# New orders for the calls of five engines in the scan part of a Mamba-2 and mixture-of-experts kernel

## The chip, the core and the metric

One core of a Trainium2 chip runs the whole program. The metric is the device time of one execution in microseconds (us). The engines are PE (TensorE, matrix products and transposes), DVE (VectorE), ACT (ScalarE), POOL (GpSimd) and SP (SyncE, which here issues most DMAs). Each engine works through its own instructions strictly in the order in which they are written; semaphores make one engine wait for another. A call that waits therefore also holds back everything written behind it on its engine.

## What is computed

Two Mamba-2 layers over 8 sequences of 512 tokens of width 256, with a residual around them and a layer norm behind, then a top-2 mixture of 8 experts. Cut to what matters here:

```python
for i in range(2):                                    # two layers
    res = h
    h = layernorm(h) * ln_w[i] + ln_b[i]
    z, xBC, dt = split(h @ in_w[i].T)
    dt = softplus(dt + dt_bias[i])
    xh, B, C = split(silu(causal_conv4(xBC) + conv_b[i]))
    # per head: state = exp(dt*A) * state + dt * x (outer) B ;  y = state . C
    y = scan(exp(dt * -exp(A_log[i])), dt, xh, B, C) + D[i] * xh
    y = y * silu(z)
    h = res + (y * rsqrt(mean(y*y) + eps) * rms_w[i]) @ out_w[i].T
x = layernorm(x + h)
x = layernorm(x + top2_experts(x))                    # 8 experts, gated by a softmax
```

## The kernel before

The scan part works in 16 **units**, one for each sequence and layer (units 0 to 7 are layer 0, 8 to 15 layer 1). A unit cuts its 512 tokens into four **chunks** `c[0]` to `c[3]` of 128 tokens; `c[4]` is chunk 0 of the next unit. While a unit's chunks are scanned, the same unit also does the input projection, convolution and layer norm of the next one (the "fills" `dt`, `c4`, `c0` to `c3`, `z0` to `z3`, `ln0`, `ln1`). Unit 0 runs the function `first`, units 1 to 8 run `plain`, units 9 to 14 run `routed`, which also routes the finished sequence to the experts (fills `t0`, `t1`, `lg`, `rk`), unit 15 runs `final`. Units 1 to 6 and 10 to 13 are loops in the program; 7, 8, 9 and 14 are written out. On every engine `plain` and `routed` are lists of calls, written by hand, and this list alone sets the order. The expert part follows from about 780 us on and isn't touched.

The calls on which the prediction rests, with the engine and the lines of the profile:

- PE `chunk_a` (L780) transposes a chunk's x into the PSUM bank `pt`; ACT `chunk_a` (L1252) copies it out to `xs`. PE `chunk_c` (L853) transposes the gated result `g` into the same bank `pt`; ACT `chunk_c` (L1257) copies the high half out, DVE `g_low` (L1678) makes the low half and frees the bank. There is one `pt`: its uses go strictly in the order a(1), c(0), a(2), c(1), a(3), c(2), a(4), c(3), each behind the one before.
- PE `chunk_cb` (L792), DVE `scan` (L1744, two instructions) and `chunk_mix` (L1752), PE `chunk_y` (L833) make the part of y from inside the chunk; PE `chunk_s` (L843) and `chunk_z` (L820), ACT `first_state` (L1315), DVE `next_state` (L1778) and `chunk_b1` (L1758) the part that comes through the state, all in the one bank `pz`. PE `chunk_d` (L871) is the output projection, ACT `chunk_d` (L1270) takes it out.
- POOL `x_dt` (L2621), `x_w` (L2629) and `x_d` (L2635) scale `xs` and so wait for ACT's copy; `old_state` (L2641); `add_xd` (L2647) adds `xd` to `y1` behind DVE `chunk_b1`. DVE `chunk_b2` (L1771) waits for `add_xd` and adds the part in PSUM. POOL `gated` (L2657) multiplies by silu(z) behind `chunk_b2`, and PE `chunk_c` waits for it.
- POOL `end` (L2584, L2585), ACT `end_scale` (L1278) and DVE `end_add` or, in plain units, `end_b` (L1719) finish the sequence of the unit before. POOL `scatter_before` (L2607) issues eight indirect DMAs in a routed unit. DVE `weigh` (L1735) and `taps` (L1705) prepare the next unit. POOL `add_x` (L2591), `rsqrt_ln` (L2578) and `u_low` (L2572) belong to the norms.
- SP loads the rows of `step_b` for each chunk (`spread_steps`, L525), which DVE `scan` waits for, and stores and loads the sequences (L550, L553, L559, L485).
- ACT functions come in table sets. `natural_log_exp_and_others` serves the softplus (L1231) and the exponentials of `steps` (L1241, L1242); the silu calls need another, and each change of set is an `ACT_TABLE_LOAD`.

## Time and profile before

| what | us |
|---|---|
| median of 3 runs (lowest, highest) | 1392.45 (1391.49, 1394.0) |
| the profiled execution | 1394.54 |
| its span, first to last instruction | 1392.5 |
| mean granted TensorE clock over the span | 0.966 |
| DVE busy, PE busy in the span | 1142.9, 1247.2 |
| a plain unit, mean of seven | 40.66 |
| a routed unit, mean of five | 46.20 |

The two unit lengths are distances between the starts of the call `weigh`, which runs once in each unit. PEclk or "clock" is the share of the full TensorE clock that was granted: 1.00 is 2.4 GHz, 0.50 is 1.2 GHz.

### The profile page before, as it was taken

The numbers are of one execution on the slowest core, as the hardware profiler recorded it, in microseconds if no ns is written. First come the engines' busy times: TensorE is split into PE (matmuls) and PEld (weight loads), VectorE is DVE, ScalarE is ACT, GpSimd is POOL, SyncE is SP. The second block draws the span as 40 slices with busy tenths as digits, with TensorE's granted clock in tenths as the row PEclk, the third lists the DMA queues.
The fourth block names the chain that finished last, engine by engine and source line by source line (L and its number), as shares of the span: only waits on it lengthen the run. The fifth ranks groups of instructions, "written<-read, shape, count | busy, mean of one in ns | idle before, by whom it ended". The sixth has DMA issues, their size and how long they took to land. (4 is left out here: it accounts for less than half of the span.)

```text
span 1392.5 us, 40595 instructions
## 1 busy us (share of the span) xinstructions
PE 1247.2 (90%) x13192; PEld 1024.2 (74%) x13193; DVE 1142.9 (82%) x2632; ACT 796.4 (57%) x1863; POOL 786.2 (56%) x743
## 2 busy tenths in 40 slices
PE   4889999999999999899977899999999999999980
PEld 2456666666666676676666789999999999999980
DVE  4889999999999999899986797869677967696656
ACT  5666666667666767576745434544545454445446
POOL 3467676677767787678776170707052707070771
PEclk9899999999999999899986999999999999999995
DMA  6213332334442323232224624232415241412554
GB/s 217 78 35 122 129 98 84 115 120 136 137 133 88 112 62 127 84 103 68 96 103 121 172 68 118 79 114 68 117 45 143 59 123 45 143 42 59 149 145 155
DMA packets 120721, 146.63 MB, mean 105 GB/s; under 512 B 47745, under 2 KB 103553, under 8 KB 120513
## 3 DMA queue, kind: packets, MB, share of 16 engines
q1 hardware_dynamic: 109504, 102.15, 24.5%
q0 software_dynamic: 10848, 42.32, 9.9%
q10 hardware_dynamic: 288, 1.19, 0.2%
q8 instruction: 39, 0.64, 0.2%
q14 instruction: 42, 0.34, 0.1%
HBM read 98.83 MB, written 37.47 MB: 98 GB/s over the span
## 5 line engine op out<-in xcount | busy, mean ns | idle before, releaser
L1111 PE MATMUL pe<-arena 128*128 128x128 f16 x3408 | 216.8, 221 | 25.7 <-issue 15.1
L1111 PEld LDWEIGHTS pe<-arena 128*128 128x128 f16 x3408 | 200.2, 99 | 33.0 <-issue 29.9
L1111 PE MATMUL pa<-arena 128*128 128x128 f16 x3408 | 215.3, 220 | 2.1 <-issue 1.1
L1111 PEld LDWEIGHTS pa<-arena 128*128 128x128 f16 x3408 | 197.9, 98 | 2.6 <-issue 1.3
L1136 PE MATMUL py<-arena 128*128 (+1 forms) x1704 | 197.6, 273 | 2.1 <-DVE arena L2363 2.1
L1572 ACT ACTIVATE arena<-pe,arena 128x128 f32<-128x128 f32 x568 | 161.2, 370 | 57.3 <-PE pe L1111 57.0
L1705 DVE SCALAR_TENSOR_TENSOR arena<-pa,arena 128x511 f32<-128x511 f32 (+2 forms) x240 | 178.7, 745 | 11.3 <-ACT arena L1209 5.2
L1136 PEld LDWEIGHTS py<-arena 128*128 128x128 f16 x1704 | 163.5, 98 | 20.3 <-issue 2.6
L1744 DVE TENSOR_TENSOR_SCAN arena<-arena,pe 128x512 f32<-128x512 f32 x128 | 148.7, 1203 | 3.2 <-issue 1.8
L2557 POOL TENSOR_SCALAR arena<-arena 128x1536 f16<-128x1536 f32 (+2 forms) x35 | 45.1, 1288 | 167.6 <-DVE arena L2363 152.5
L833 PEld LDWEIGHTS py<-arena 128*128 128x128 f32 x1024 | 124.2, 197 | 17.9 <-issue 9.1
L833 PE MATMUL py<-arena 128*128 128x64 f32 x1024 | 129.5, 281 | 1.5 <-DVE arena L1752 1.0
L686 PE MATMUL pa<-arena 128*128 128x512 f16 x480 | 120.9, 393 | 9.6 <-DVE arena L1705 9.5
L2657 POOL TENSOR_TENSOR arena<-arena 128x512 f32<-128x512 f32 x64 | 88.5, 1383 | 66.5 <-DVE arena L1771 66.4
L2315 DVE SCALAR_TENSOR_TENSOR pm<-pa,arena 128x128 f32<-128x128 f32 x284 | 80.3, 350 | 52.5 <-ACT arena L1572 48.7
L1578 ACT ACTIVATE arena<-pm 128x512 f16<-128x512 f32 x71 | 42.4, 597 | 131.0 <-DVE pm L2315 131.0
L2315 DVE SCALAR_TENSOR_TENSOR pz<-pa,arena 128x128 f32<-128x128 f32 x284 | 80.3, 351 | 32.9 <-ACT arena L1572 32.0
L871 PE MATMUL pm<-arena 128*128 128x256 f16 x768 | 100.2, 283 | 7.8 <-DVE arena L1678 7.1
L1578 ACT ACTIVATE arena<-pz 128x512 f16<-128x512 f32 x71 | 42.4, 597 | 111.6 <-DVE pz L2315 111.6
L694 PE MATMUL pa<-arena 128*128 128x512 f16 x384 | 95.0, 390 | 3.4 <-ACT arena L1198 2.0
L871 PEld LDWEIGHTS pm<-arena 128*128 128x128 f16 x768 | 76.6, 102 | 25.6 <-DVE arena L1678 10.2
L2847 POOL DMA_INDIRECT arena<-answer,arena x64 | 61.2, 956 | 54.6 <-issue 54.6
(306 smaller groups left out, 2535.8 us busy)
## 6 DMA issues: line engine op xcount, KB each, us to landing
arena<-step_rows SPq DMA_DIRECT2D x64, 512.0 KB, 6.0
arena<-in_w_exp POOLq DMA_DIRECT2D x32, 768.0 KB, 4.9
arena<-queue SPq DMA_DIRECT2D x74, 129.5 KB
answer<-arena SPq DMA_DIRECT2D x71, 128.0 KB, 1.7
arena<-in_x SPq DMA_DIRECT2D x16, 512.0 KB, 6.5
answer<-zeros SPq DMA_DIRECT2D x10, 512.0 KB, 4.8
arena<-h SPq DMA_DIRECT2D x9, 512.0 KB, 6.1
h<-arena SPq DMA_DIRECT2D x8, 512.0 KB, 3.0
```

What stands on the lines that cost most here:

```text
L686: ins = pe.matmul(bank[:, :], win[:, l, b, d, OX + c * P:OX + (c + 1) * P], uT[:, vq, a, d, :], start=(n == 0), stop=(n == len(passes) - 1))
L694: ins = pe.matmul(bank[:, :], uT[:, vq, a, d, k * P:(k + 1) * P], win[:, l, b, d, 0:DI], start=(n == 0), stop=(n == len(passes) - 1))
L833: ins = pe.matmul(py[:, h * HD:(h + 1) * HD], mix[:, kq, h, :], dtx[:, kq, h, :], start=True, stop=True)
L871: ins = pe.matmul(OUT, gT[:, c.kq, a, t, :], wout[:, c.layer, b, t, :], start=(n == 0), stop=(n == len(passes) - 1))
L1111: ins = pe.matmul(bank[:, f * P:(f + 1) * P], w_split[:, p, hl, d * 2 * FF + col:d * 2 * FF + col + P], x_hl[:, r, x, d * P:(d + 1) * P], ...
L1136: ins = pe.matmul(py[:, 0:D], a[:, b, f, :], part(p, hl, W1N + f * D, D), start=(half == 0 and n == 0), stop=(half == 1 and n == len(passe ...
L1572: ins = e.activation(sg[:, half, f, :], GATE[half][:, f * P:(f + 1) * P], ACT.Silu, bias=b1a[:, bass.ds(ex_, 1), ff], scale=1.0 / S1)
L1578: e.activation(acth[:, r, 4 * half:4 * half + 4].rearrange("p f t -> p (f t)"), GLU[half][:, :], ACT.Copy).then_inc(hi_done[half], 1)
L1705: ins = dve.scalar_tensor_tensor(acc[:, mq, s:T], pa[bank][:, 0:T - s], cw[:, l, ct, TAPS - 1 - s:TAPS - s], acc[:, mq, s:T], ALU.mult, AL ...
L1744: dve.tensor_tensor_scan(flat[:, h * T:(h + 1) * T], step_b[:, c.k, h * T:(h + 1) * T], IDENT4[:, :], 0.0, ALU.mult, ALU.add).then_inc(sca ...
L2315: ins = dve.scalar_tensor_tensor(GLU[half][:, f * P:(f + 1) * P], VALUE[half][:, f * P:(f + 1) * P], b1v[:, bass.ds(ex_, 1), ff], sg[:, ha ...
L2657: pool.tensor_tensor(g[:, kq], y2[:, kq], zs[:, c.q, k].rearrange("p (h d) -> p h d", h=NH), ALU.mult).then_inc(g_ready, 1)
```

## The change

The lists `plain` and `routed` get new orders on all five engines. SP's loop over the units is taken apart into `first_unit`, `plain_unit` and `routed_unit` for this. No call does other work; three waits are added where the new orders need them (ACT `chunk_a` also waits for `dtx_ready` and `xw_ready`, POOL `x_d` waits for ACT's copy itself), and the loading of the logarithm table becomes a call of its own, `log_table`. The core of the diff, with both lists of POOL whole:

```diff
@@ SP, plain_unit @@
+                store_steps(u + 1)
+                load_hres(u)
+                if u + 3 <= MAMBA_UNITS:
+                    load_hln(u + 3)
+                clear(u)
+                spread_steps(u + 1, 0)
+                store_h(u)
+                spread_steps(u + 1, 1)
+                spread_steps(u + 1, 2)
+                store_hx(u)
+                spread_steps(u + 1, 3)
@@ PE, plain @@
+                chunk_cb(c[2])
+                chunk_c(c[0])
                 do_fills(st, ["c1"])
-                chunk_c(c[0])
-                chunk_s(c[1])
                 chunk_y(c[1])
                 do_fills(st, ["c2"])
+                chunk_d(c[0])
+                chunk_cb(c[3])
                 chunk_a(c[2])
-                chunk_z(c[2])
-                chunk_d(c[0])
-                chunk_cb(c[2])
-                do_fills(st, ["c3"])
-                chunk_s(c[2])
+                chunk_s(c[1])
                 turn_b(st.u + 1, 1 - st.q, c[0].n + 1)
                 chunk_c(c[1])
...
@@ PE, routed @@
+                chunk_y(c[0])
+                chunk_cb(c[2])
+                chunk_a(c[1])
+                do_fills(st, ["c0"])
+                chunk_c(c[0])
+                do_fills(st, ["c1"])
+                steps(st.u + 1, 1 - st.q)
+                chunk_z(c[1])
...
@@ ACT, routed @@
+                first_state(c[0])
+                log_table()
+                conv_first(st, "c4")
+                chunk_a(c[1])
+                softplus(st)
+                conv_first(st, "c0")
+                end_scale(st)
+                chunk_c(c[0])
+                conv_silu(st, "c4")
+                conv_silu(st, "c0")
+                steps(st)
+                conv_first(st, "c1")
+                chunk_a(c[2])
+                conv_first(st, "c2")
+                conv_silu(st, "c1")
...
@@ DVE, plain @@
+                ln_stats(st.u + 2, st.h + 1, st.q)
                 scan(c[1])
                 dt_first(st)
                 chunk_mix(c[1])
+                chunk_b2(c[0])
...
+                scan(c[2])
+                g_low(c[0])
+                chunk_mix(c[2])
+                chunk_b2(c[1])
+                taps(st, "c1", ch1)
+                next_state(c[1])
+                taps(st, "c2", ch1)
+                chunk_b1(c[2])
+                taps(st, "c3", ch1)
+                ch1.close()
                 weigh(st)
+                g_low(c[1])
+                next_state(c[2])
+                chunk_b2(c[2])
...
@@ DVE, routed @@
+                taps(st, "c0", ch1)
+                end_add(st)
+                chunk_b1(c[1])
...
+                chunk_mix(c[4])
                 g_low(c[3])
-                chunk_mix(c[4])
+                weigh(st)
@@ POOL, x_d @@
                 n, kq = c.n, c.kq
+                pool.wait_ge(pt_free, c.use("a") + 1)
                 at_least(pool, y_free, n - 1)
@@ POOL, plain @@
-                x_d(c[1])
-                add_xd(c[1])
-                old_state(c[2])
-                gated(c[1])
-                x_w(c[2])
-                x_dt(c[2])
-                add_x(st)
-                x_d(c[2])
...
+                old_state(c[1])
+                end(st)
                 gated(c[0])
                 x_dt(c[1])
+                x_w(c[1])
+                rsqrt_ln(st.u + 2)
                 x_d(c[1])
+                x_d(c[2])
                 add_xd(c[1])
+                gated(c[1])
+                x_dt(c[2])
+                x_w(c[2])
                 old_state(c[2])
+                x_d(c[3])
                 add_xd(c[2])
                 gated(c[2])
                 x_dt(c[3])
                 add_xd(c[3])
                 gated(c[3])
                 x_w(c[4])
                 x_dt(c[4])
                 u_low(st.u + 2, st.q, st, "ln0")
                 u_low(st.u + 2, st.q, st, "ln1")
+                add_x(st)
+                x_d(c[4])
@@ POOL, routed @@
+                x_d(c[1])
+                scatter_before(st, 0, 1)
+                end(st)
+                old_state(c[1])
+                gated(c[0])
+                add_xd(c[1])
+                x_dt(c[1])
+                x_w(c[1])
+                scatter_before(st, 1, 2)
+                x_d(c[2])
+                rsqrt_x1(st)
+                x_dt(c[2])
+                gated(c[1])
...
+                add_xd(c[3])
+                x_d(c[4])
+                scatter_before(st, 6, 7)
+                scatter_before(st, 7, 8)
+                gated(c[3])
+                u_low(st.u + 2, st.q, st, "ln0")
+                u_low(st.u + 2, st.q, st, "ln1")
+                x_w(c[4])
+                x_dt(c[4])
```

How the instructions stand before and after, at three places. The lines of the kernel after are shifted by 45 to 54.

**POOL in unit 8, the last plain one, before.** From `gated` of chunk 0 on:

```order
L2657 TENSOR_TENSOR arena<-arena 128x512 [waits pt_free,ss_ready,y_free]
L2621 TENSOR_TENSOR arena<-arena 128x512 [waits y_full,pt_free]
L2635 TENSOR_TENSOR arena<-arena 128x512 [waits y_free]
L2647 TENSOR_TENSOR arena<-arena 128x512 [waits xd_ready,z_free]
L2641 TENSOR_TENSOR arena<-arena 128x256 [waits z_free]
L2657 TENSOR_TENSOR arena<-arena 128x512 [waits pt_free,ss_ready,y_free]
L2629 TENSOR_TENSOR arena<-arena 128x512 [waits z_full,wdt_ready,pt_free]
L2621 TENSOR_TENSOR arena<-arena 128x512 [waits y_full,pt_free]
L2591 TENSOR_TENSOR arena<-arena 128x1024 [waits h_ready]
L2635 TENSOR_TENSOR arena<-arena 128x512 [waits y_free]
```

The same stretch of POOL after the change (`gated` is L2712 now, `x_dt` L2675, `x_w` L2683, `rsqrt_ln` L2632, `x_d` L2690, `add_xd` L2702, `old_state` L2696):

```order
L2712 TENSOR_TENSOR arena<-arena 128x512 [waits pt_free,ss_ready,y_free]
L2675 TENSOR_TENSOR arena<-arena 128x512 [waits y_full,pt_free]
L2683 TENSOR_TENSOR arena<-arena 128x512 [waits z_full,wdt_ready,pt_free]
L2632 TENSOR_TENSOR arena<-arena,half_neg 128x4 [waits ln_done,ln_var]
L2633 TENSOR_TENSOR arena<-arena 128x4 [waits ln_pow]
L2690 TENSOR_TENSOR arena<-arena 128x512 [waits y_free,pt_free] x2
L2702 TENSOR_TENSOR arena<-arena 128x512 [waits xd_ready,z_free]
L2712 TENSOR_TENSOR arena<-arena 128x512 [waits pt_free,ss_ready,y_free]
L2675 TENSOR_TENSOR arena<-arena 128x512 [waits y_full,pt_free]
L2683 TENSOR_TENSOR arena<-arena 128x512 [waits z_full,wdt_ready,pt_free]
L2696 TENSOR_TENSOR arena<-arena 128x256 [waits z_free]
```

`x_d` of chunks 1 and 2 now stand together ahead of `add_xd` of chunk 1; before, `x_d` of chunk 2 stood six calls behind it.

**PE in unit 8, before** (`chunk_c` of chunk 0, `chunk_s`, `chunk_y`, the fill `c2`, `chunk_a` of chunk 2):

```order
L853 MATMUL pt<-ident,arena 128x128 [waits pt_free,g_ready]
L853 MATMUL pt<-ident,arena 128x128 x3
L843 MATMUL pz<-arena 64x256 [waits bs_ready,z_free,xw_ready]
L843 MATMUL pz<-arena 64x256
L833 MATMUL py<-arena 128x64 [waits y_free,dtx_ready,m_done]
L833 MATMUL py<-arena 128x64 x7
L686 MATMUL pa0<-arena 128x512 [waits a_free0]
L686 MATMUL pa0<-arena 128x512 x5
L780 MATMUL pt<-ident,arena 128x128 [waits pt_free]
```

and after (`chunk_y`, the fill, `chunk_d` of chunk 0, `chunk_cb` of chunk 3, `chunk_a` of chunk 2, `chunk_s`):

```order
L878 MATMUL py<-arena 128x64 [waits y_free,dtx_ready,m_done]
L878 MATMUL py<-arena 128x64 x7
L731 MATMUL pa0<-arena 128x512 [waits a_free0]
L731 MATMUL pa0<-arena 128x512 x5
L916 MATMUL pm<-arena 128x256 [waits ex_ready,out_free,pt_free]
L916 MATMUL pm<-arena 128x256 x11
L837 MATMUL pe0<-arena 128x128 [waits m_done]
L825 MATMUL pt<-ident,arena 128x128 [waits pt_free]
L825 MATMUL pt<-ident,arena 128x128 x3
L888 MATMUL pz<-arena 64x256 [waits bs_ready,z_free,xw_ready]
```

`chunk_d` of chunk 0 and a `chunk_cb` now stand ahead of `chunk_a` of chunk 2.

**POOL at the start of unit 14, the last routed one, before** (`end`, three scatters, `x_w`, `x_dt`, `gated` of chunk 0):

```order
L2584 TENSOR_SCALAR arena<-arena 128x4 [waits ss_ready]
L2585 TENSOR_TENSOR arena<-arena,half_neg 128x4 [waits sve_ready]
L2607 DMA queue<-arena 34304x259 [waits slot_ready,x1_ready]
L2607 DMA queue<-arena 34304x259 x2
L2629 TENSOR_TENSOR arena<-arena 128x512 [waits z_full,wdt_ready,pt_free]
L2621 TENSOR_TENSOR arena<-arena 128x512 [waits y_full,pt_free]
L2657 TENSOR_TENSOR arena<-arena 128x512 [waits pt_free,ss_ready,y_free]
```

and after:

```order
L2690 TENSOR_TENSOR arena<-arena 128x512 [waits y_free,pt_free]
L2661 DMA queue<-arena 34304x259 [waits slot_ready,x1_ready]
L2638 TENSOR_SCALAR arena<-arena 128x4 [waits ss_ready]
L2639 TENSOR_TENSOR arena<-arena,half_neg 128x4 [waits sve_ready]
L2696 TENSOR_TENSOR arena<-arena 128x256 [waits z_free]
L2712 TENSOR_TENSOR arena<-arena 128x512 [waits pt_free,ss_ready,y_free]
L2702 TENSOR_TENSOR arena<-arena 128x512 [waits xd_ready,z_free]
L2675 TENSOR_TENSOR arena<-arena 128x512 [waits y_full,pt_free]
L2683 TENSOR_TENSOR arena<-arena 128x512 [waits z_full,wdt_ready,pt_free]
```

`x_d` of chunk 1 (it waits for ACT's copy of that chunk) now stands ahead of `end`, and `add_xd` of chunk 1 ahead of `x_dt`.

## Rows read from the trace of the kernel before

**Rows 1.** Busy time by unit: length; PE, PEld, DVE, ACT, POOL; clock, DMA, GB/s.

```profile
271.95:313.02 41.07, 38.53 (x277) 26.80 (x277) 38.21 (x61) 26.46 (x53) 28.32 (x28) 1.00 0.37 115
...
483.97:528.86 44.89, 41.61 (x306) 30.25 (x306) 42.63 (x111) 31.31 (x63) 36.06 (x36) 1.00 0.31 105
528.86:579.39 50.53, 45.16 (x302) 32.48 (x301) 43.51 (x110) 30.69 (x62) 35.98 (x36) 0.90 0.35 112
```

**Rows 2.** DVE `weigh` in time order: start, us, instruction; first and last of each stretch.

```profile
108.93 0.33 DVE L1735 TENSOR_TENSOR arena<-arena 128x32 f32<-128x32 f32 x1 [0.40 <-ACT arena L1242]
...
393.52 0.40 DVE L1735 TENSOR_TENSOR arena<-arena 128x32 f32<-128x32 f32 x1 [0.17 <-ACT arena L1242]
439.14 0.18 DVE L1735 TENSOR_TENSOR arena<-arena 128x32 f32<-128x32 f32 x1
...
670.12 0.18 DVE L1735 TENSOR_TENSOR arena<-arena 128x32 f32<-128x32 f32 x1
```

**Rows 3.** A plain unit in time order, single calls of DVE, PE, ACT, POOL.

```profile
274.55 0.68 DVE L1678 SCALAR_TENSOR_TENSOR arena<-pt,arena 128x512 f16<-128x512 f32 x1
281.12 1.21 DVE L1752 TENSOR_TENSOR arena<-arena,pe 128x1024 f32<-128x1024 f32 x1
...
275.29 0.65 PE L780 MATMUL pt<-ident,arena 128*128 128x128 f32 x4 [0.72 <-DVE arena L1678]
...
277.18 1.47 PE L871 MATMUL pm<-arena 128*128 128x256 f16 x12
278.59 0.48 PE L792 MATMUL pe<-arena 64*128 64x128 f32 x2
...
276.11 0.59 ACT L1252 ACTIVATE arena<-pt 128x512 f32<-128x512 f32 x1
...
270.93 1.04 POOL L2635 TENSOR_TENSOR arena<-arena 128x512 f32<-128x512 f32 x1
285.87 1.28 POOL L2647 TENSOR_TENSOR arena<-arena 128x512 f32<-128x512 f32 x1
```

**Rows 4.** DVE `taps` and `scan`, 100 to 500 us: busy us, mean ns | idle.

```profile
L1705 DVE SCALAR_TENSOR_TENSOR arena<-pa,arena 128x511 f32<-128x511 f32 x150 | 111.6, 744 | 3.7
L1744 DVE TENSOR_TENSOR_SCAN arena<-arena,pe 128x512 f32<-128x512 f32 x76 | 88.3, 1202 | 0.7
```

**Rows 5.** Routed units in time order: POOL scatter and `end`, PE, ACT `end_scale`.

```profile
475.81 1.01 POOL L2607 DMA_INDIRECT queue<-arena  x1 [0.16 <-issue]
...
510.17 1.49 PE L871 MATMUL pm<-arena 128*128 128x256 f16 x12 [0.99 <-DVE arena L1678]
...
516.86 1.46 PE L686 MATMUL pa<-arena 128*128 128x512 f16 x6
...
511.49 1.04 POOL L2585 TENSOR_TENSOR arena<-arena,half_neg 128x4 f32<-128x4 f32 x1
...
515.85 1.71 ACT L1278 ACTIVATE arena<-arena 128x256 f32<-128x256 f32 x4
```

**Rows 6.** ACT, a change of table set in a plain unit, and what follows.

```profile
271.68 1.28 ACT L1220 ACT_TABLE_LOAD   x1
272.97 0.63 ACT L1220 ACTIVATE arena<-arena 64x512 f32<-64x512 f32 x1
```

**Rows 7.** PE's idle stretches in time order, with their length in brackets.

```profile
91.48 0.66 PE L853 MATMUL pt<-ident,arena 128*128 128x128 f32 x4 [2.27 <-POOL arena L2657]
...
568.40 1.11 PE L853 MATMUL pt<-ident,arena 128*128 128x128 f32 x4 [2.61 <-POOL arena L2657]
...
706.25 1.09 PE L709 MATMUL pa<-ident,arena 128*128 128x128 f32 x8 [2.73 <-DVE arena L1728]
```

**Rows 8.** One-us stretches for PE: busy, granted clock, DMA, GB/s.

```profile
567.00:568.00 1.00, 0.00 (x0) 0.73 0.00 0
...
577.00:578.00 1.00, 1.00 (x8) 0.65 0.94 350
```

**Rows 9.** DMA issues by kind: KB each, median us to landing.

```profile
arena<-step_rows SPq DMA_DIRECT2D x64, 512.0 KB, 6.0
```

More of the change, by code:

```diff
@@ L1358, in first @@
                 chunk_a(c[1])
+                log_table()
                 softplus(st)
@@ new lines, in plain @@
+                taps(st, "c1", ch1)
[4 more added lines that the diff above has]
+                ch1.close()
+                weigh(st)
+                g_low(c[1])
+                next_state(c[2])
+                chunk_b2(c[2])
+                scan(c[3])
+                chunk_b1(c[3])
+                chunk_mix(c[3])
+                end_b(st)
+                chunk_b2(c[3])
+                g_low(c[2])
@@ new lines, in plain, with routed @@
+                scan(c[4])
+                chunk_mix(c[4])
+                g_low(c[3])
+            def routed(st):
+                c = [Chunk(st, k) for k in range(NK + 1)]
+                scan(c[1])
+                chunk_mix(c[1])
+                dt_first(st)
+                scan(c[2])
+                chunk_b2(c[0])
+                ch1 = Chain(dve, c_dve2, S1_LINKS, st.u + 1)
+                taps(st, "c4", ch1)
+                dt_last(st, ch1)
+                taps(st, "c0", ch1)
+                end_add(st)
+                chunk_b1(c[1])
+                ch3 = s3_stats(st)
@@ L2014, in plain @@
+                scan(c[3])
+                next_state(c[2])
                 chunk_b2(c[2])
-                next_state(c[2])
-                scan(c[3])
                 chunk_mix(c[3])
+                s3_top(st, ch3)
                 chunk_b1(c[3])
+                s3_place(st, ch3)
                 g_low(c[2])
@@ L2021, in plain @@
                 scan(c[4])
+                chunk_mix(c[4])
                 g_low(c[3])
[L2023 to L2062 removed]
+                weigh(st)
             def final(st):
@@ L2772, in routed @@
                 x_dt(c[4])
-                x_d(c[4])
                 u_low(st.u + 2, st.q, st, "ln0")
                 u_low(st.u + 2, st.q, st, "ln1")
+                add_x(st)
+                x_d(c[4])
+            def routed(st):
+                c = [Chunk(st, k) for k in range(NK + 1)]
+                x_d(c[1])
[11 more added lines that the diff above has]
+                gated(c[1])
+                scatter_before(st, 2, 3)
+                x_w(c[2])
+                rsqrt_ln(st.u + 2)
+                old_state(c[2])
+                scatter_before(st, 3, 4)
+                add_xd(c[2])
+                gated(c[2])
+                scatter_before(st, 4, 5)
+                x_dt(c[3])
+                x_d(c[3])
+                scatter_before(st, 5, 6)
+                add_xd(c[3])
[7 more added lines that the diff above has]
+                x_dt(c[4])
             def final(st):
```

350 lines of the change are left out of this document (138 added, 212 removed).

## The prediction, written before the result was known

> **What bounds the kernel now.** I read the busy times by unit first. A plain unit is 41.07 us long; DVE is busy for 38.21 of it and PE for 38.53, at clock 1.00 [rows 1]. A routed unit is 44.89 with DVE at 42.63 and PE at 41.61 [rows 1]. So two engines are nearly full, and together with the strict order on each engine that bounds the gain from above and leaves the loss open: DVE has 2.86 us of idle time in a plain unit and 2.26 in a routed one, and a new order can take away no more than that, but can add any wait. The starts of `weigh` give the lengths: 7 plain units in 393.52 - 108.93 = 284.59, 40.66 each, and 5 routed ones in 670.12 - 439.14 = 230.98, 46.20 each [rows 2]. One of the five is 50.53 with clock 0.90, where the others are near 45 [rows 1].
>
> I lay the new lists against each other, each call with its duration from a row, counting time from the first DVE call of a unit. What has to be looked for is a call that now stands behind another that waits for something later.
>
> **Plain units, first wait.** POOL's `add_xd` of chunk 1 now stands behind `x_d` of chunk 2, which needs ACT's copy of chunk 2. PE's `chunk_a` of chunk 2 waits for the bank `pt`, which DVE `g_low` of chunk 0 frees, and on PE `chunk_d` of chunk 0 (it waits for the same `g_low`) and a `chunk_cb` now stand ahead of it. From the start of `g_low`: 0.68, then PE 1.47 + 0.48 + 0.65, ACT's copy 0.59, `x_d` 1.04, `add_xd` 1.28 [rows 3], 6.2 in all, and with some 0.05 for each of five hand-overs (PE starts 0.06 after `g_low` ends, 274.55 + 0.68 against 275.29 [rows 3]) 6.4. DVE has only `g_low` and `chunk_mix`, 0.68 + 1.21 [rows 3], less a small overlap, to do before `chunk_b2` of chunk 1, which waits for `add_xd`: 1.8. **DVE waits 4.6.**
>
> **Second wait.** The same pattern for chunk 2: `add_xd` stands behind `x_d` of chunk 3, whose `chunk_a` waits for `g_low` of chunk 1, with nothing ahead of it this time: 0.68 + 0.65 + 0.59 + 1.04 + 1.28 = 4.2 [rows 3], 4.5 with hand-overs; DVE has `g_low` and `next_state`, 0.9. **3.6.** Elsewhere in the unit I find 0.4 (the first `taps` wait for `conv_first`, since PE has `chunk_s` and `chunk_y` ahead of the fill `c4`). DVE's calls keep their time, so the unit is 41.07 - 2.86 + 4.6 + 3.6 + 0.4 + 0.3 (its waits for its own results) = 47.1; the 0.8 that every second unit is shorter goes half into the waits, and I take 47.0 for all. Eight units: 8 x (47.0 - 40.66) = **+51**.
>
> **SP** now issues the step rows of chunks 1 and 2 behind the store of h, which waits for `end_b`. They land 6.0 later [rows 9]. From the end of `end_b` to the next `scan` of chunk 1 DVE has `chunk_b2`, two `g_low`, a scan pair, `chunk_mix` and `ln_stats`, 7.5 by my layout, and SP needs 0.8 to get to them. That hides them by 0.7; a landing 2 us late would cost 1.3 in each of eight units, +10, which I keep for the range. `weigh` and `add_x` move to late places, where nobody waits for them.
>
> **Routed units, first wait.** POOL now begins with `x_d` of chunk 1, so a scatter, `end`, `old_state` and `gated` of chunk 0 all stand behind ACT's copy of chunk 1. On PE the seven calls from `chunk_d` to `chunk_y` take 516.86 - 510.17 = 6.7 [rows 5]; `chunk_cb` and the transpose behind them and ACT's copy bring the copy to 8.0. Then `x_d` 1.0, a scatter 1.2, `end` 1.3 and ACT's `end_scale` 1.71 [rows 3, 5]: ready at 13.6. DVE has until `end_add` two scan pairs, one `chunk_mix`, two `taps` of three instructions (1.20 and 0.74 each [rows 4]) and small calls: 11.9. **DVE waits 1.8.**
>
> **Second.** `gated` of chunk 0 is done at 13.8 (`end` 11.9, `old_state` 0.6, 1.28 [rows 3]). PE has had nothing to do since the fill `c0` at 8.7, because `chunk_c` of chunk 0 is next: **5.2 us idle**. Behind it stand the fill `c1`, `steps` and `chunk_z`, some 3.7 more. `chunk_b1` of chunk 1 starts at 17.7 where DVE was ready at 14.8. **2.9.** `gated` of chunk 1 likewise sits behind `x_d` of chunk 2 and `x_dt`, which leaves PE idle for 2.9.
>
> **Third.** At the end `gated` of chunk 3 stands behind `x_d` of chunk 4 and two scatters. The copy of chunk 4, behind ACT's `ln_out`, is there at 49.7; + 1.0 + 2 x 1.2 + 1.3, + PE 0.65, + ACT 0.6 with hand-overs gives `g_low` of chunk 3 at 56.2, where DVE was done at 51.5. **4.7**, with PE idle for 4.6. Four small waits (`chunk_mix`, `g_low` and `chunk_b1` of chunk 1 and 2, `s3_place`) add 2.7. Sum 12.1, and 44.89 + 12.1 = 57.0; unit 9 has no scatters, 3.6 less. Six units: 5 x 57.0 + 53.4 - 6 x 46.20 = **+61**. If all of the idle 2.26 went, 14 less.
>
> **ACT's tables.** In `routed` the exponentials of `steps` now stand between silu calls: two more loads in each unit, 2 x 1.28 [rows 6]. `conv_first` of `c1` is ready at 21.4 by my layout and DVE comes to it at 22.3, so they are hidden, with 0.9 to spare; without that cover they are 2.6 x 6 = 15. The row after a load starts 0.01 behind its end [rows 6]. The Trainium skill (ScalarE: Activation LUTs, "What ACT_TABLE_LOAD costs") adds a drain of about 1.38 to each switch; by that rule the sum would be some 19 us more (an estimate from that page: 1.0 in each plain unit, 1.9 in each routed one). The row shows no drain, and I go by the row.
>
> **The clock.** This is the second large term. When PE had been idle for 2.61 and for 2.73, the clock fell to 0.50 [rows 7]; after the first it fell in 567 to 568 and came back in 577 to 578, with PE busy throughout from 568.4 [rows 7, 8]. After 2.27 it did not fall [rows 7]. The unit of the first fall took 50.53 against 44.89, 5.6 more [rows 1]. The new lists leave PE idle for 4.7 in each plain unit (from `turn_b` to `chunk_c` of chunk 1, through the first wait), and for 5.2, 2.9 and 4.6 in each routed one. Each fall makes PE's work of the next 7 to 9 us twice as long, and behind all of these gaps it is on the path to DVE's next call. I take 3.5 for a plain unit (PE's calls up to `chunk_a` of chunk 3, 7 us, at half speed for 7) and 2 x 3.7 for a routed one, leaving the gap of 2.9 out: 8 x 3.5 + 6 x 7.4 = **+72**.
>
> **Sum.** 51 + 61 + 72 = +184 on the profiled execution's 1394.54: 1578.5. The median of the runs is 2.1 below it, so **1576**.
>
> **The rivals.**
> *The clock holds.* The waits are as above, but no gap meets the clock's fall. For: a gap of 2.27 went by without one [rows 7]. Against: both gaps over 2.6 shown did not, and these are up to twice as long. It gives 1392 + 112 = 1504.
> *More falls.* The routed gap of 2.9 also counts (4.3 x 6 = 26) and PE's two gaps around `chunk_c` of chunk 2 in a plain unit, 1.6 and 1.8 with little between, bring a second fall there (4.4 x 8 = 35): 1602 to 1637.
> *Faster.* The point is POOL's `x_d` of chunk 2 in plain units. If the copy of chunk 2 is there when POOL comes to it, `add_xd` isn't late, DVE's idle 2.86 shrinks to its own 0.4 in each plain unit, and the routed units keep their length: 8 x -2.4 = -19, 1373. It decides where the wait at `chunk_b2` of chunk 1 is under 2.9; I get 4.6 from durations alone, with one `pt` bank, so this needs an error of mine in the order.
> *The waits overlap.* In a chain of five engines a wait may take the place of a later one; with half of the waits gone and no fall of the clock it is about 1450.
>
> **How the numbers follow.** 0.60 for the forecast, 0.17 for the clock that holds, 0.14 for more falls, 0.04 for faster or no change, 0.05 for overlapping waits. The forecast's own terms carry an error of 1.5 us in each unit, +-20. The range reaches from the second case less 14 to the lower half of the third: 1490 to 1630. 0.2% is 2.8 us, about what a measurement of this kernel can tell from no change. Faster 0.03, same 0.01, slower 0.96.
>
> **What would show it.** In the profile after: `weigh` 50 to 51 us apart in plain units and 64 in routed ones (47 and 57 with the clock at 1.00); DVE's largest wait is `chunk_b2` for `add_xd`, some 8 us in each plain unit; `g_low` for ACT and `chunk_b1` for PE in routed units; PE's idle time before `chunk_c` for `gated`, 4 to 5 us at a time; a clock clearly under 0.97 between 100 and 800 us; the expert part as long as before. Wrong would be: `add_xd` without a late `x_d` ahead of it, DVE still 90% busy in plain units, or a clock of 1.00 behind gaps of 4 us.

## The result, and the profile of the changed kernel

The changed kernel takes 1562.9 us (median of 4 runs, 1562.4 to 1565.3), the kernel before, on the same chip, 1393.2: a ratio of 1.122, 95% interval 1.120 to 1.124. The forecast was 1576 with a range of 1490 to 1630. The profiled execution took 1562.42 with a span of 1560.7. In the later comparisons the kernel before had 1393.3 to 1394.1.

The page of the changed kernel: busy time of each engine, and the granted clock in 40 slices of the span.

```profile
PE 1312.3 (84%) x13192; PEld 1070.8 (69%) x13193; DVE 1155.6 (74%) x2632; ACT 819.3 (52%) x1875; POOL 779.4 (50%) x743
...
PEclk9998898988898999887888869999999999999996
```

The kernel before has 1247.2 for PE, 1142.9 for DVE and 796.4 for ACT. PE's matmuls are longer at the lower clock; ACT has 12 more instructions, the table loads (15 us); DVE has the same 2632 instructions and is busy for 12.7 more, 9.1 of it in the two small instructions of `ln_stats` that the last section is about; the rest is a balance of other small ones. Of the first 24 digits 15 are under 9, where 4 were: the falls lie in the scan part; the expert part behind them is as it was, 638.3 from its first product to the end in both kernels. The 170 us came mostly as waits. The engines by stretch, a plain unit and three of the five routed ones (length; busy PE, and in the plain unit PEld, DVE, ACT, POOL too; clock, DMA share, GB/s), which answer to [rows 1]:

```profile
275.85:326.94 51.09, 43.24 (x278) 30.52 (x277) 37.18 (x61) 27.43 (x53) 28.10 (x27) 0.87 0.29 93
...
552.53:611.63 59.10, 45.01 (x306) 0.90 0.23 82
611.63:671.81 60.18, 47.14 (x309) 0.87 0.23 80
671.81:737.45 65.64, 51.09 (x309) 0.81 0.20 65
```

`weigh` starts seven periods from 125.12 to 480.04, 50.70 us each (before 40.66), and five from 552.53 to 863.51, 62.2 each (before 46.2 [rows 2]). The routed units come in two lengths, 59.1 to 60.3 three times and 65.6 and 65.8, and the longer ones have the lower clock (0.81 and 0.79).

DVE's waits in the plain unit from 275.85 to 326.94, summed by pair (total, times, longest); before, the largest wait of this kind was under 1 us:

```profile
DVE arena L1825 <- POOL arena L2702: 8.0, 2, 4.5
DVE arena L1732 <- ACT arena L1307: 2.0, 1, 2.0
DVE arena L1812 <- PE pz L865: 1.8, 1, 1.8
DVE arena L1825 <- PE py L878: 1.3, 1, 1.3
```

One unit from its chunk 1 to its chunk 3, across the late `weigh` at 275.85, first POOL, then DVE, then PE (start, length, instruction, idle time in front of it and its releaser). L2690 is `x_d` of chunk 2 and L1302 ACT's copy of that chunk, L2702 `add_xd`, L2712 `gated`; L1825 is `chunk_b2`, L1812 `chunk_b1`, L1806 `chunk_mix`, L1732 `g_low` and L1307 ACT's `chunk_c`; L898 is PE's `chunk_c`, L878 `chunk_y`, L865 `chunk_z`:

```profile
263.51 1.04 POOL L2690 TENSOR_TENSOR arena<-arena 128x512 f32<-128x512 f32 x1 [5.84 <-ACT arena L1302]
...
265.81 0.69 DVE L1825 TENSOR_TENSOR arena<-py,arena 128x512 f32<-128x512 f32 x1 [4.50 <-POOL arena L2702]
273.01 0.69 DVE L1812 TENSOR_TENSOR arena<-pz,arena 128x512 f32<-128x512 f32 x1 [1.74 <-PE pz L865]
280.44 0.69 DVE L1825 TENSOR_TENSOR arena<-py,arena 128x512 f32<-128x512 f32 x1 [3.48 <-POOL arena L2702]
288.15 0.69 DVE L1825 TENSOR_TENSOR arena<-py,arena 128x512 f32<-128x512 f32 x1 [1.30 <-PE py L878]
295.07 0.69 DVE L1732 SCALAR_TENSOR_TENSOR arena<-pt,arena 128x512 f16<-128x512 f32 x1 [1.96 <-ACT arena L1307]
...
268.06 1.11 PE L898 MATMUL pt<-ident,arena 128*128 128x128 f32 x4 [4.36 <-POOL arena L2712]
282.68 0.65 PE L898 MATMUL pt<-ident,arena 128*128 128x128 f32 x4 [1.45 <-POOL arena L2712]
285.13 2.89 PE L878 MATMUL py<-arena 128*128 128x64 f32 x16 [1.79 <-DVE arena L1806]
```

And PE's granted clock around them, in stretches of 3 us (length, PE busy, clock, DMA share, GB/s):

```profile
265.00:268.00 3.00, 0.00 (x0) 0.59 0.00 0
268.00:271.00 3.00, 2.94 (x9) 0.50 0.00 0
271.00:274.00 3.00, 3.00 (x12) 0.77 0.00 0
274.00:277.00 3.00, 3.00 (x25) 1.00 0.00 0
...
283.00:286.00 3.00, 1.21 (x12) 1.00 0.00 0
286.00:289.00 3.00, 3.00 (x17) 0.50 0.39 137
...
292.00:295.00 3.00, 3.00 (x24) 0.86 0.34 137
```

POOL's `x_d` of chunk 2 waits 5.84 for ACT's copy, `add_xd` of chunk 1 runs behind it (264.51 to 265.77), and `chunk_b2` starts at 265.81. PE stands still for 4.36 us and its clock falls from the 2.4 to the 1.2 GHz level; it stands still for 1.45 and 1.79 with one short call between, and the clock falls again. The waits for PE and ACT (1.74, 1.30, 1.96) stand behind the falls, each of those for POOL (4.50, 3.48) ahead of one.

A routed unit, in the same form; L1782 is `end_add`, L1328 ACT's `end_scale`, L837 `chunk_cb`:

```profile
615.71 1.22 DVE L1806 TENSOR_TENSOR arena<-arena,pe 128x1024 f32<-128x1024 f32 x1 [1.65 <-PE pe L837]
626.69 1.23 DVE L1782 TENSOR_TENSOR arena<-arena 128x1024 f32<-128x1024 f32 x1 [1.80 <-ACT arena L1328]
632.31 0.69 DVE L1812 TENSOR_TENSOR arena<-pz,arena 128x512 f32<-128x512 f32 x1 [4.40 <-PE pz L865]
671.20 0.69 DVE L1732 SCALAR_TENSOR_TENSOR arena<-pt,arena 128x512 f16<-128x512 f32 x1 [4.80 <-ACT arena L1307]
...
626.66 1.11 PE L898 MATMUL pt<-ident,arena 128*128 128x128 f32 x4 [4.97 <-POOL arena L2712]
635.53 1.97 PE L878 MATMUL py<-arena 128*128 128x64 f32 x16 [1.97 <-issue]
643.76 0.66 PE L898 MATMUL pt<-ident,arena 128*128 128x128 f32 x4 [1.54 <-POOL arena L2712]
669.42 1.11 PE L898 MATMUL pt<-ident,arena 128*128 128x128 f32 x4 [4.57 <-POOL arena L2712]
```

### The profile page after: what moved, and what is told of

Its sections match the earlier page's. It is cut to its first block and busy times, and to the rows that moved or that the text cites. A ratio compares the mean times of both kernels' runs of the same rounds, so it can differ in the third digit from the quotient of the medians.

```text
span 1560.7 us, 40707 instructions
## 1 busy us (share of the span) xinstructions
PE 1312.3 (84%) x13192; PEld 1070.8 (69%) x13193; DVE 1155.6 (74%) x2632; ACT 819.3 (52%) x1875; POOL 779.4 (50%) x743
## 5 line engine op out<-in xcount | busy, mean ns | idle before, releaser
L878 PE MATMUL py<-arena 128*128 128x64 f32 x1024 | 139.7, 295 | 25.8 <-DVE arena L1806 14.7
L878 PEld LDWEIGHTS py<-arena 128*128 128x128 f32 x1024 | 134.6, 210 | 37.2 <-issue 17.6
L2690 POOL TENSOR_TENSOR arena<-arena 128x512 f32<-128x512 f32 x64 | 66.6, 1041 | 184.4 <-ACT arena L1302 184.4
L898 PE MATMUL pt<-ident,arena 128*128 128x128 f32 x256 | 50.2, 329 | 119.3 <-POOL arena L2712 118.2
L731 PE MATMUL pa<-arena 128*128 128x512 f16 x480 | 138.4, 432 | 2.0 <-DVE arena L1759 2.0
L898 PEld LDWEIGHTS pt<-ident,arena 128*128 128x128 f32 x256 | 33.6, 165 | 132.8 <-issue 88.4
L916 PE MATMUL pm<-arena 128*128 128x256 f16 x768 | 119.1, 317 | 6.0 <-DVE arena L1732 5.7
L2369 DVE SCALAR_TENSOR_TENSOR pm<-pa,arena 128x128 f32<-128x128 f32 x284 | 80.2, 350 | 52.7 <-ACT arena L1626 49.2
L2712 POOL TENSOR_TENSOR arena<-arena 128x512 f32<-128x512 f32 x64 | 83.3, 1301 | 63.4 <-DVE arena L1825 63.1
L916 PEld LDWEIGHTS pm<-arena 128*128 128x128 f16 x768 | 87.8, 117 | 34.3 <-DVE arena L1732 12.1
L1825 DVE TENSOR_TENSOR arena<-py,arena 128x512 f32<-128x512 f32 x64 | 43.9, 686 | 81.6 <-POOL arena L2702 66.8
```

The lines of the kernel that those rows point to most:

```text
L731: ins = pe.matmul(bank[:, :], win[:, l, b, d, OX + c * P:OX + (c + 1) * P], uT[:, vq, a, d, :], start=(n == 0), stop=(n == len(passes) - 1))
L878: ins = pe.matmul(py[:, h * HD:(h + 1) * HD], mix[:, kq, h, :], dtx[:, kq, h, :], start=True, stop=True)
L898: ins = pe.transpose(pt[:, t * P:(t + 1) * P], gk[:, t * P:(t + 1) * P], ident[:, :])
L916: ins = pe.matmul(OUT, gT[:, c.kq, a, t, :], wout[:, c.layer, b, t, :], start=(n == 0), stop=(n == len(passes) - 1))
L2369: ins = dve.scalar_tensor_tensor(GLU[half][:, f * P:(f + 1) * P], VALUE[half][:, f * P:(f + 1) * P], b1v[:, bass.ds(ex_, 1), ff], sg[:, ha ...
L2690: pool.tensor_tensor(xd[:, kq], xs[:, kq], by_head(dsk[:, c.layer]), ALU.mult).then_inc(xd_ready, 1)
```

## The experiments

The theory is that of the prediction: a call of POOL that waits for a late copy of ACT now stands ahead of one that others need, PE idles behind it, its clock falls, and DVE waits again for the slower PE. What has to be told apart is which kind of unit pays, whether POOL's order alone does it, and how much is the clock's.

### One kind of unit alone

The first run has the old lists of all engines in routed units, the second has them in plain units; the other kind is new.

> The kernel after, with all five lists of the routed units in their old order; the plain units keep the new one. My theory (each kind of unit has waits and falls of the clock of its own, about 10.0 us in each of 8 plain units, 16 in each of 6 routed ones as the two traces put them, 50.7 against 40.7 and 62.2 against 46.2): plain units stay at 50 to 51, routed ones go back to 45 to 46, time 1393 + 80 = 1473 (1465 to 1482). Rival, that the kinds of unit feed each other's delays across their border (calls of chunk 4 are late, the clock stays low): the routed units stay above 50 and the time is above 1500.

> The kernel after, with all five lists of the plain units in their old order; the routed units keep the new one. My theory: plain units 40.7, routed ones 62, time 1393 + 6 x 16, less a little for unit 9, = 1483 (1472 to 1492), and what this and the kernel with plain units alone lose sums to the whole loss of 170 within 6. Rival, feeding across the border: the two losses sum to clearly less or more than 170.

Measured: 1471.0 (ratio 1.055, 1.053 to 1.057) and 1482.9 (1.065, 1.063 to 1.067). The two losses, 77.7 and 89.7, add up to 167.4, where both together lose 169.6. Within these intervals the two losses simply add: eight plain units lose 9.7 us each, six routed ones 15.0. (That an edit of one kind can still change single units of the other shows further down.)

### POOL's two calls in plain units, taken back and put in

In the first kernel only POOL's list of plain units is edited, all else is the changed kernel:

```
                 x_d(c[1])
-                x_d(c[2])
                 add_xd(c[1])
                 gated(c[1])
+                x_d(c[2])
...
-                x_d(c[3])
                 add_xd(c[2])
                 gated(c[2])
+                x_d(c[3])
```

> The kernel after with one change: in POOL's plain list x_d of chunk 2 and of chunk 3 stand behind add_xd and gated of the chunk before, not ahead of them; all other lists as they are. My theory (these two calls make DVE wait 4.0 twice, and the PE gap behind the first brings the fall of the clock): both waits of DVE for add_xd fall to under 1, the clock is 1.00 in plain units, a plain unit goes from 50.7 to 39.5 to 42.5, time 1563 - 8 x 9.5 = 1487 (1475 to 1505). Rival one, PE's order is the cause (chunk_d and chunk_cb ahead of chunk_a): the wait moves to another call (x_dt for chunk_y, gated for chunk_c) and the unit stays above 47, time above 1530. Rival two, the new DVE order with end_b late and ln_stats first: the unit stays near 50.

Measured: 1487.1 (1.068, 1.063 to 1.074), 76 below the changed kernel and the time of the run with only the routed units new. A plain unit of it (columns as above):

```profile
241.48:282.43 40.95, 38.39 (x277) 26.71 (x277) 39.75 (x61) 27.01 (x53) 28.03 (x27) 1.00 0.36 116
```

The clock is at 1.00 and DVE waits for POOL no more. The second kernel is the kernel before, with the one edit the other way round:

```
                 x_d(c[1])
+                x_d(c[2])
                 add_xd(c[1])
...
                 add_x(st)
-                x_d(c[2])
```

> The kernel before with one edit, on POOL in plain units: x_d of chunk 2 ahead of add_xd of chunk 1 (and the wait on pt_free in front of it, which x_dt had done for it). Theory (the order of POOL alone makes the first wait): add_xd(1) now queues behind a copy of xs that ACT makes only after PE's taps, so DVE's chunk_b2(1) waits 3.5 to 4.5 us where it waited none, PE gets a gap of 4 us or more ahead of chunk_c(1) and the granted clock falls behind it; plain units go from 40.7 to 43.7 to 47, the time to 1415 to 1443. Rival (the wait needs the new order of the other engines too, which reach chunk_a(2) later in the new plain unit): under 1 us per unit, at most 1400.

Measured: 1440.3 (1.033, 1.031 to 1.035), plain units 46.0 to 47.6. POOL, DVE and PE in it (L2636 is `x_d`, L2648 `add_xd`, L1771 `chunk_b2`, L820 `chunk_z`), and PE's clock:

```profile
300.97 1.04 POOL L2636 TENSOR_TENSOR arena<-arena 128x512 f32<-128x512 f32 x1 [4.80 <-ACT arena L1252]
301.97 1.26 POOL L2648 TENSOR_TENSOR arena<-arena 128x512 f32<-128x512 f32 x1
...
303.26 0.69 DVE L1771 TENSOR_TENSOR arena<-py,arena 128x512 f32<-128x512 f32 x1 [4.87 <-POOL arena L2648]
...
304.34 1.95 PE L820 MATMUL pz<-arena 128*128 128x256 f32 x4 [5.15 <-DVE arena L1778]
...
301.00:304.00 3.00, 0.00 (x0) 1.00 0.55 171
...
305.00:308.00 3.00, 3.00 (x14) 0.51 0.00 0
```

The whole chain stands here in five rows: `x_d` waits 4.80 for the copy, `add_xd` runs behind it, `chunk_b2` waits 4.87, PE 5.15, and then the clock falls. PE's gap is ahead of `chunk_z`, not of `chunk_c` as I had written. One call too early costs 6 us in each of eight units, in a kernel that is otherwise as it was. PE's new order, whose `chunk_d` and `chunk_cb` the forecast counts ahead of the copy, is not needed for it.

### The clock by itself

The changed kernel with matmuls whose results nobody reads, so that PE doesn't idle; no wait is taken away. In the first kernel 34 of them (128x256) stand behind `turn_b`, in the second also 10 ahead of `chunk_c(c[2])` and 14 ahead of `chunk_y(c[3])`.

```
                 turn_b(st.u + 1, 1 - st.q, c[0].n + 1)
+                filler(34)
                 chunk_c(c[1])
...
+                filler_c(c[2], 10)
                 chunk_c(c[2])
+                filler_y(c[3], 14)
                 chunk_y(c[3])
```

> The kernel after with 34 matrix products of 128x256 f16 (about 0.11 us each at the full clock, 3.7 in all) added on PE in each plain unit, behind turn_b and ahead of chunk_c of chunk 1, which is where PE is idle for 4.4; their results go to a part of a PSUM bank that nobody reads. They separate the wait from the clock. My theory: the clock stays at 1.00 in plain units where the gap of 4.4 alone made it fall, a plain unit goes from 50.7 to 47 to 48, time 1563 - 8 x 3.5 = 1535 (1525 to 1547). Rival, the clock costs nothing here since DVE waits for POOL anyway: 1563 within 5. If the falls come from the later gaps instead, the clock stays low and the time too: 1555 to 1570.

> The changed kernel with matmuls whose results nobody reads in plain units, in the three gaps of TensorE: 34 (128x256) behind turn_b, 10 ahead of chunk_c(2), 14 ahead of chunk_y(3). Nothing is taken from any wait. Theory: the two falls of the granted clock in a plain unit come of the gaps; with all three filled the clock stays at its upper level and the unit is 50.7 less 1.7 (the wait for chunk_z) and less 2.5 to 3.3 (the waits for chunk_y(3) and chunk_c(3)): 46 to 47, the time 1520 to 1535 (with the first gap alone filled it was 1550.6 at 47.9). Rival (the second pair of waits is the order's, not the clock's): it stays at 47.9 and 1550.

Measured: 1550.6 (1.110, 1.105 to 1.116) and 1562.5 (1.120, 1.118 to 1.122). Units of the first and of the second kernel, in the columns of [rows 1]; the last two lines are routed ones of the second:

```profile
223.04:270.93 47.89, 43.48 (x311) 31.10 (x311) 37.18 (x60) 27.25 (x53) 28.01 (x27) 0.96 0.32 99
...
272.76:320.81 48.05, 45.07 (x335) 32.26 (x335) 38.52 (x60) 27.12 (x53) 28.01 (x27) 1.00 0.31 99
...
610.55:675.76 65.21, 50.88 (x309) 36.49 (x307) 44.46 (x111) 34.43 (x65) 35.31 (x36) 0.81 0.21 74
675.76:736.40 60.64, 47.45 (x309) 33.48 (x307) 45.13 (x111) 34.50 (x65) 35.31 (x36) 0.87 0.21 70
```

The fillers did in most units to the clock what they should. With the first alone one fall is left in six of the seven units counted. With all three none is left in four of the seven, and the waits of 1.74, 1.30 and 1.96 are gone there but for 0.4; the other three still show one fall (clock 0.93 to 0.97), without an idle stretch of PE over 1 us ahead of it. In the unit shown two waits over half a microsecond are left at the clock of 1.00, 3.73 and 4.51, both for `add_xd`: these are the order's own.

But this unit takes 48.05 and the mean of the seven is 49.2 (48.0 to 51.0), where 46 to 47 was expected. The three waits had made 5.0; DVE is busy for 1.3 more than in the changed kernel's unit (the last section tells where), the waits for `add_xd` have grown by 0.3, and small gaps by 0.5. And the time is not lower, because the routed units, whose code is not touched, took 60.6 once and 64.3 to 65.5 four times, where the changed kernel has three near 60 and two near 66. So the rival's number came (1562.5, even above its 1550), but not by its reason.

The 1535 expected of the first kernel was too low because five of its units take 47.9, 2.8 less than the mean of 50.7 and not 3.5, and the other two 49.5 and 50.7.

### POOL's order in routed units

The start of the unit:

```
+                end(st)
+                old_state(c[1])
+                gated(c[0])
                 x_d(c[1])
                 scatter_before(st, 0, 1)
-                end(st)
-                old_state(c[1])
-                gated(c[0])
                 add_xd(c[1])
```

> The changed kernel with POOL's routed unit re-ordered at its start: end, old_state and gated(0) first, then x_d(1) and the scatter. Theory: end_add's wait (1.80 us) and the PE gap ahead of chunk_c(0) (4.97) go, with them the fall of the clock behind the gap and so most of DVE's wait for chunk_z at chunk_b1(1) (4.40): routed units 62.2 -> 56 to 58, the time 1526 to 1540. Rival (PE has other work to catch up, so chunk_z still is late, or the time comes back at the third wait): 1550 to 1563.

Measured: 1524.8 (1.093, 1.092 to 1.095), 38 lower. Routed units are 53.1 to 56.5 long instead of 62.2; the wait at `end_add` is gone, and that at `chunk_b1` of chunk 1 too, where it was 3.8 to 5.6. In the first of the five, DVE instead waits 1.51 for ACT's `conv_first` and 0.93 for `chunk_z` at `chunk_b1` of chunk 2. The end of the unit:

```
+                gated(c[3])
                 x_d(c[4])
                 scatter_before(st, 6, 7)
                 scatter_before(st, 7, 8)
-                gated(c[3])
```

> The changed kernel with gated(3) on POOL in routed units ahead of x_d(4) and the last two scatters. Theory: DVE's wait of 4.4 to 4.8 us at g_low(3) shrinks to under 1 us and PE's gap of 4.6 ahead of chunk_c(3) goes: 62.2 -> 57 to 58 per routed unit, the time 1532 to 1542. Rival (what is saved there is waited for at the start of the next unit, since x_d(4), its x_w and x_dt and the scatters come that much later): 1555 to 1563.

Measured: 1554.8 (1.113, 1.108 to 1.117), 8 lower where the full wait would be 29. The rival's range, 1555 to 1563, begins just above it. PE of this kernel at the head of one unit, and further on DVE (L2626 is POOL's `u_low`):

```profile
615.09 0.76 PE L723 MATMUL pa<-arena 128*128 128x8 f16 x24 [1.97 <-POOL arena L2626]
...
616.00:621.00 5.00, 5.00 (x17) 0.50 0.01 3
621.00:626.00 5.00, 5.00 (x21) 0.50 0.00 0
...
657.71 0.69 DVE L1812 TENSOR_TENSOR arena<-pz,arena 128x512 f32<-128x512 f32 x1 [3.64 <-PE pz L865]
```

The wait of 4.8 at `g_low` is gone, as meant. But `u_low` now is late for PE's fill `dt`, the clock falls there, and further on DVE waits 3.64 for `chunk_z` at `chunk_b1` of chunk 2, behind a fall that lasts 11 us in both units of this kernel that I read. In the changed kernel such a long one stands in the unit of 65.64 but not in that of 60.18. What was saved at the end of one unit is largely waited for in the next: units of 58.9, 64.9, 61.0, 61.8, 56.7.

All three edits of POOL together, the other engines' new lists kept:

> The changed kernel with all three repairs of POOL's order together: in plain units x_d(2) and x_d(3) behind add_xd and gated of the chunk before; in routed units end and gated(0) ahead of x_d(1), and gated(3) ahead of x_d(4). The other four engines keep the new order. Theory (nearly all of the loss is POOL's order and the falls of the clock behind its gaps): the two single repairs that worked add up, 1562.9 less 76 less 38 = 1449, and the third brings 8 (what it brought alone) to 29 (its full wait): 1420 to 1441. Rival (the second half of the routed unit is set by other things, as when the third repair stood alone): 1441 to 1455.

Measured: 1423.7 (1.020, 1.018 to 1.023). POOL's calls in four places, and the falls of the clock behind them, make 139 of the 170 us. Together the three bring more than each alone: 76 + 38 + 8 would be 1441, and 17 more came. Which pair of them does that was not tried. The rest, 30 us, is in the routed units (48.9 to 53.8, before 46.2), where DVE's waits for PE are 3.3 at most; what makes it was not tried.

### What the new plain units are worth without that fault

> The new plain units with POOL's x_d(2) and x_d(3) moved back, and the old routed units on all engines. By adding up the single runs: 1471 less 76 = 1395, the same as the kernel before (plain units 41.0 where the kernel before has 40.7).

> As the run with the repaired plain units and the old routed ones, and besides the two small tensor_scalar (128x4) that end ln_stats on DVE are made on POOL, ahead of the pow that reads them. In the repaired plain unit these two took 2.37 and 1.08 us on DVE, each ending with the POOL instruction (add_x 2.36, x_d 1.03) that had begun 0.02 us before or stood behind it, where in the kernel before they took 0.17 each. Theory (they stand still for POOL's instruction, which costs DVE 3.1 us in each unit): DVE busy 39.75 -> 36.6 per plain unit, the unit 41.0 -> 39 to 40 (PE's 38.4 and its gaps are next), the time 8 to 16 us below the run without this edit, some 1380 to 1388 and so below the kernel before. Rival (DVE's time there is covered by PE, or POOL's own row gets longer and gated later): within 3 us of the run without this edit.

> The kernel before, its own order throughout, with the same edit that made the repaired units shorter: the two small tensor_scalar of ln_stats made on POOL. Theory (the edit pays only where DVE reaches them while POOL is in a long instruction): in the kernel before they took 0.17 each in all 14 units, so DVE gains 0.15 per unit and POOL loses 0.3 to 0.5 that it has idle; within 4 us of the kernel before, plain units 40.3 to 41.1 as they are. Rival (these two were in the way in every order): 8 to 18 us faster, as it was in the repaired order.

The first, repaired plain units and the old routed ones, takes 1392.2 (0.9985, 0.9973 to 0.9996), the same as the kernel before. In its plain units DVE and POOL show this (L2645 `add_x`, L2690 `x_d`, L1721 and L1722 the last two instructions of `ln_stats`):

```profile
259.78 2.38 DVE L1721 TENSOR_SCALAR arena<-arena 128x4 f32<-128x4 f32 x1
262.07 1.08 DVE L1722 TENSOR_SCALAR arena<-arena 128x4 f32<-128x4 f32 x1
...
259.77 2.36 POOL L2645 TENSOR_TENSOR arena<-arena 128x1024 f32<-128x1024 f32 x1
262.08 1.04 POOL L2690 TENSOR_TENSOR arena<-arena 128x512 f32<-128x512 f32 x1
```

Two instructions on four elements per partition end with the POOL instructions beside them (262.16 and 262.13, 263.15 and 263.12). No view of waits counts this, since the time is recorded as busy. In the kernel before they take 0.17 and 0.16 in every unit. The edit makes them on POOL, where `rsqrt_ln` reads them; DVE's wait for `ln_rs` moves a few calls up with it:

```
-                dve.tensor_scalar(nm, mv[:, :, 0], -1.0, None, ALU.mult)
-                dve.tensor_scalar(ve, mv[:, :, 1], EPS, None, ALU.add).then_inc(ln_var, 1)
+                dve.sem_inc(ln_var, 1)
...
+                pool.tensor_scalar(nm, mv[:, :, 0], -1.0, 0.0, ALU.mult, ALU.add)
+                link(pool.tensor_scalar(ve, mv[:, :, 1], 1.0, EPS, ALU.mult, ALU.add), ln_pow, 2 * w)
```

Measured: **1375.2 us (0.986, 0.984 to 0.988), faster than both kernels**, 1.4% below the kernel before. Its plain unit, and below it that of the run without the edit:

```profile
274.55:312.86 38.31, 37.81 (x277) 26.88 (x277) 36.95 (x58) 27.25 (x53) 28.47 (x29) 1.00 0.38 124
...
244.10:285.05 40.95, 38.39 (x277) 26.70 (x277) 39.74 (x60) 27.02 (x53) 28.05 (x27) 1.00 0.36 116
```

DVE's busy time falls by 2.8, the unit by 2.6, and PE is now busy for 37.81 of 38.31: it is the bound. The same edit in the kernel before takes 1393.5 (1.0005, 0.9991 to 1.0018), units of 40.4 to 41.5: nothing. The gain needs the new order and the edit together.

## Why the prediction was right, and where it was not

**Plain units, first and second wait.** Forecast 4.6 and 3.6, measured 4.50 and 3.48, at the places named, with PE idle 4.36 where 4.7 was forecast. Laying the lists against each other with durations from single rows was enough. The run that takes the two calls back and the one that puts one of them in show the cause. The second also shows the wait (4.87) without PE's new order, which the forecast had as a part of it.

**Length of a plain unit.** Forecast 47.0 by waits and 3.5 by the clock, 50.5 in all; measured 50.70. That this came so close is in part luck. In the means of the seven units DVE is busy for 37.6, where the forecast kept its 38.2, and waits 8.0 for POOL, where it had 8.2; the waits for PE and ACT behind the falls are 4.3 and not 3.5, small gaps 0.8. The clock's term failed in its number of falls too: I took one, and there are two. The second, behind the gaps of 1.45 and 1.79 around `chunk_c` of chunk 2, stood in the rival of more falls at 4.4 on top of the first's 3.5. In the units shown DVE waits only 1.74 behind the first, since PE catches up ahead of the second wait, which holds DVE anyway; behind the second 3.3. Too few falls and too high a price for each cancelled. What the unit would take with the clock at 1.00 and nothing else changed no run shows: the fillers' 48.05 holds 1.3 of DVE standing still for POOL, which the changed kernel's unit has not (last section).

**Routed units.** `end_add` 1.8 forecast and 1.80 measured in the unit shown (1.6 to 2.0 in the five); PE idle 5.2 and 4.97, 4.6 and 4.57; `g_low` of chunk 3 4.7 and 4.4 to 5.1. `chunk_b1` of chunk 1 was forecast at 2.9 before the clock and is 4.40 with it, so by this difference the first fall costs 1.5 and not 3.7; behind the one at the unit's end DVE waits 1.65 at `chunk_mix`, not 3.7. In all 64.4 was forecast and 62.2 measured. The mis-sized term is the clock's, two falls at 3.7 each: a fall's cost ends at the next wait that stands anyway.

Two things that the forecast didn't have stand against that. DVE is busy for 44.5 on average and not 42.6, 1.1 of it in the two small instructions of `ln_stats`. And each of the five units has a third fall, between the two forecast ones. In the three units near 60 it lasts 4 us and begins 1 to 2 us behind the end of a gap of 1.96 or 1.97 ahead of `chunk_y` of chunk 1. I had no term for that gap: `chunk_y` needs `x_dt`, which on POOL now stands behind `add_xd` of chunk 1 and ends at 635.43, 0.10 ahead of `chunk_y` (the profile names no releaser, so this is read from the times and the order). In the two near 66 it lasts 11 us, behind gaps of 2.56 and 2.27 ahead of `chunk_c` of chunk 1, the place that I had left out with 2.9; there DVE waits 3.6 and 3.7 more for `chunk_z`.

**Sum.** Forecast +184. In the runs of one kind alone +78 for plain units (forecast 51 + 28 = 79) and +90 for routed ones (61 + 44 = 105). The miss of 14 us is all in the routed term, and by the two waits just given in the clock's part of it; DVE's longer busy time and the third fall make it smaller than that part alone would.

**SP, the tables.** No wait of `scan` for the step rows shows in the units read. The table loads of the changed kernel's scan part start at most 0.03 behind the ACT instruction before them, and the next one starts 0.01 to 0.02 after the load's end (616.71 + 1.28 against 618.00), as in [rows 6], but for eight that wait for DVE. With a drain of about 1.38 on each switch (the Trainium skill, ScalarE: Activation LUTs, "What ACT_TABLE_LOAD costs") the forecast would have been an estimated 1595, further off; no load here shows one. That the loads are hidden is read from the trace and was not tried by itself.

**The rivals.** A clock that holds is excluded by the rows. Of the further falls in the rival of more falls the plain one came in every unit counted and the routed one in two of five; its 1602 to 1637 was still too high, since its prices were, like the forecast's own. The point that I named for the faster case was the right one: with `x_d` of chunks 2 and 3 behind `add_xd` the unit is 40.95 long and the run as a whole level with the kernel before. That it didn't come out shorter, as that rival had it (8 x -2.4), is the two small instructions; with them away the plain units are 2.4 shorter than before. That this is the rival's figure is chance: it had DVE full but for 0.4, and here DVE is idle for 1.36 of 38.31, PE sets the length, and DVE's busy time is 1.3 shorter than before.

## What to carry to other kernels

In an engine's list look for the call that waits longest for others, and then at what stands behind it: one `x_d` of 1.04 us, put ahead of the `add_xd` that DVE needs, cost 6 us a unit. Where a gap on PE lets the clock fall, count what stands until the next wait that is there anyway, and look for falls behind short gaps too. And when a tiny instruction of DVE has a long busy time in one order and not in another, look at what POOL runs at that moment: that time hides in "busy", and moving two instructions of 0.17 us was worth 17.

## What the runs showed of the hardware

**DVE standing still for POOL.** A `tensor_scalar` of 128x4 float32 from and to SBUF took 0.17 beside an idle POOL and 2.37 beside a POOL instruction of 2.36, ending with it; its successor took 1.08 beside the next one of 1.04. The Trainium skill (SBUF — State Buffer, "Who interferes with whom") says that a `tensor_scalar` of DVE can need the pair of ports that DVE and GpSimd share, and that whoever issues first then has it for the whole instruction, while the other is blocked. The traces agree: POOL's start is 259.77 and DVE's 259.78; and in the changed kernel, where DVE's starts at 145.59 and POOL's of 2.36 at 145.61, DVE's keeps its 0.16. Starts this close can't be told apart always (262.07 for the blocked successor, 262.08 for POOL's).

In the twelve traces in which DVE makes these two, all 112 of them that took over 0.25 us ended at most 0.05 behind the end of a POOL instruction. One that is blocked need not be let in at the first end: in the changed kernel one began at 644.18 beside a scatter that ended at 644.86, and ended at 645.98, 0.04 behind the `x_w` that POOL began at 644.89. DVE's instructions with a PSUM operand in the same units (`scan`, `taps`) kept their length beside POOL.

This standing still was not in my sum. In the changed kernel the first of the two has a median of 0.33 in plain units, but 1.80 in the routed unit from 611.63; in the run with all fillers it took 2.35 to 2.37 in all seven plain units. In the unit shown of that run the two make 2.2 more of busy time, other small instructions 0.9 less, which gives the 1.3: there it begins at 291.86, 0.01 behind POOL's `add_x`, where in the changed kernel's unit it began at 297.64, 0.09 ahead of it, and took 0.17.

**The clock.** It fell behind single gaps of 4.36, 4.97 and 4.57, and also behind 1.45 and 1.79 close together, both shorter than the 2.27 behind which it had stayed up [rows 7]. How long it stays down differs for the same code. Here is PE's clock, us by us, at the end of the middle fall of the changed kernel's unit of 60.18, and at the start and the end of that in the unit of 65.64:

```profile
638.00:639.00 1.00, 1.00 (x6) 0.50 1.01 348
641.00:642.00 1.00, 1.00 (x6) 0.99 1.06 358
...
706.00:707.00 1.00, 1.00 (x4) 0.50 0.58 199
716.00:717.00 1.00, 1.00 (x8) 0.95 0.00 0
```

The first lasts from 637.5 to 641, the second from 705.5 to 716.5. Every routed unit of this kernel has three falls; by this middle one those near 66 differ from those near 60, and which came changed when only plain units were edited, with the fillers. In the other runs there are lengths between (59.1 to 64.1 with the routed units alone new). Nor does a fall need a long gap, or cost time: with the three repairs six of seven plain units show one of 4 us, five of them without an idle stretch of PE over 1 us in the unit up to there, and the units are 40.9 long on average; with the same plain code and the changed routed units the clock stayed at 1.00, at 41.0. What decides it is left open; an edit that takes one fall away may bring another further on.
